# A state-space, expert and attention kernel: early expert loads, woven row sums, reordered attention steps

## The reference, cut to what matters

```
def step(h, inp):
    x_t, dt_t, B_t, C_t = inp
    h = exp(dt_t[..., None] * A[None]) * h + dt_t[..., None] * B_t[:, None, :] * x_t[..., None]
    return h, einsum('bdn,bn->bd', h, C_t) + D_param * x_t
x = x + ssm(xn) + weight[:, None] * expert_of_token(xn)      # layer 0, top 1 of 8
xn = layernorm(x)
scores = g * sem_scores + (1.0 - g) * geo_scores             # layer 1, causal, 16 heads
x = x + softmax(scores) @ v @ wo + shared(xn) + routed_experts(xn)
```

## Time and profile before

| what | value |
|---|---|
| median of 3 runs | 1795.22 us (1791.27 to 1803.44) |
| profiled execution | 1794.59 us, of which 1793.0 us are the span |
| PE busy / PEld busy | 1685.1 us (94%) / 1363.9 us (76%) |
| DVE / ACT / POOL busy | 1181.0 (66%) / 1024.4 (57%) / 784.1 us (44%) |
| granted TensorE clock, mean | 0.975 of 2.4 GHz |
| state steps, about | 77 to 250 us |
| layer-0 experts | 250 to 327 us |
| attention | 367 to 1370 us |
| layer-1 experts and shared expert | 1370 to 1793 us |

### The profile page before, as it was taken

The page is one execution under the profiler, slowest core; times in us unless marked ns, Lnnn a source line. Parts: engine busy times, 40 slices in busy tenths (PEclk is TensorE's granted clock), DMA queues, the critical chain, the costliest instruction groups (busy, mean ns, idle before and its releaser), DMA issues. The chain is left out here.

```text
span 1793.0 us, 33443 instructions
## 1 busy us (share of the span) xinstructions
PE 1685.1 (94%) x9234; PEld 1363.9 (76%) x9234; DVE 1181.0 (66%) x2391; ACT 1024.4 (57%) x2303; POOL 784.1 (44%) x805
## 2 busy tenths in 40 slices
PE   6499989489999999999999999999997999999998
PEld 3365657378888888888888888888886777777787
DVE  6889863687887766766767667667663444344487
ACT  6699934166665656665666666566653444444332
POOL 2599952453334443434443444434550333222374
PEclk9599999699999999999999999999999999999999
DMA  3232339400090100000000000001004999999633
GB/s 127 81 107 94 105 109 309 144 7 1 16 371 11 39 13 22 21 6 26 15 12 20 19 7 29 12 20 38 28 25 151 320 324 313 315 323 322 196 112 100
DMA packets 102555, 193.29 MB, mean 108 GB/s; under 512 B 15700, under 2 KB 59988, under 8 KB 101828
## 3 DMA queue, kind: packets, MB, share of 16 engines
q1 hardware_dynamic: 63300, 125.02, 21.7%
q0 software_dynamic: 17152, 47.67, 8.0%
q10 hardware_dynamic: 22032, 19.73, 3.5%
HBM read 140.84 MB, written 51.51 MB: 107 GB/s over the span
## 5 line engine op out<-in xcount | busy, mean ns | idle before, releaser
L1437 POOL TENSOR_TENSOR sw<-sw,rope_t 64x512 f32<-64x512 f32 x128 | 166.7, 1302 | 521.9 <-ACT sw L1050 492.6
L1079 ACT ACTIVATE pb<-ps,negmax 128x128 f32<-128x128 f32 (+7 forms) x256 | 190.8, 745 | 151.7 <-DVE negmax L1290 150.0
L965 PEld LDWEIGHTS ps<-pt,v 128*128 128x128 f32 x1280 | 242.0, 189 | 42.0 <-DVE xr L1318 4.0
L965 PE MATMUL ps<-pt,v 128*128 128x256 f32 (+1 forms) x1280 | 270.7, 358 | 2.8 <-DVE xr L1318 2.6
L563 POOL DMA_DIRECT2D w2r<-in_w x148 | 77.2, 522 | 314.9 <-PE ps L612 271.4
L1290 DVE TENSOR_REDUCE negmax<-ps 128x1 f32<-128x128 f32 (+7 forms) x256 | 194.0, 758 | 8.8
L646 DVE SCALAR_TENSOR_TENSOR ga<-th,ps 128x176 f32<-128x176 f32 x148 | 50.0, 338 | 225.7 <-ACT th L627 225.7
L1066 ACT COPY pt<-ps 128x512 f32<-128x512 f32 (+3 forms) x384 | 171.6, 484 | 38.7 <-PE ps L955 35.6
L1440 POOL TENSOR_TENSOR t<-t,sw 64x512 f32<-64x512 f32 x128 | 167.8, 1311 | 17.8 <-POOL sw L1437 12.8
L595 PE MATMUL ps<-w13r,xt 128*128 128x352 f32 x496 | 168.6, 463 | 0.0
L955 PE MATMUL ps<-ident,pb 128*128 128x128 f32 x1152 | 167.5, 272 | 0.0
(11 more groups left out here) (246 smaller groups left out, 4000.7 us busy)
## 6 DMA issues: line engine op xcount, KB each, us to landing
w13r<-in_w SPq DMA_DIRECT2D x124, 352.0 KB, 4.8
w2r<-in_w POOLq DMA_DIRECT2D x148, 176.0 KB, 4.8
result<-yy ACTq DMA_DIRECT2D x148, 128.0 KB, 4.5
crow<-c_rows SPq DMA_DIRECT2D x32, 512.0 KB, 3.6
sorted<-zero_tile SPq DMA_DIRECT2D x31, 512.0 KB, 6.1
t<-sorted SPq DMA_DIRECT2D x124, 128.0 KB, 4.0
hc<-in_w SPq DMA_DIRECT2D x24, 352.0 KB, 5.5
wraw<-in_wqk SPq DMA_DIRECT2D x16, 256.0 KB, 2.7
```

The source lines that it names most:

```text
L965: last = pe.matmul(ps[:, 6, c0:2 * P], v[:, j, hd], pt[g % 2][:, j, c0:2 * P], start=j == 0, stop=j == 2 * g + 1)
L1079: act.activation(pb[:, qt % 2, 0:cols], ps[:, bank:bank + 2, :].rearrange("p a n -> p (a n)")[:, 0:cols], ACT.Exp, bias=negmax[:, par, qn: ...
L1437: g.tensor_tensor(sw[64:128, p % 2, :], sw[64:128, p % 2, :], rope_t[64:128, 1, (p // 2) * 512:(p // 2 + 1) * 512], ALU.mult).then_inc(s_t ...
```

## The change

It has three parts, and removes or adds no arithmetic.

1. **Memory and loads.** The layer-0 `w13` ring gets memory of its own, at the end of the stack; the token ring now lies in `zeros`, the tile that the zero fill of `sorted0` reads. SP waits for that fill (R0.zeroed) in place of s_ysum, and makes the table's round trip after the first pair of state steps.
2. **Row sums.** Before the experts nothing is transposed back. The 8 groups stand at the end of the expert steps s = 2 to 7 (one each in 2 to 5, two each in 6 and 7), on TensorE and on VectorE; the wait for s_yT stands at the end of step 1.
3. **Attention.** In odd steps of a first head TensorE makes `values` before `project_out`, and VectorE copies the values before `add_out`. In even steps of a second head VectorE does `output` before `turned`.

```
-        shared_memory = {
-            'w13r0': hc_flat[:, 0:w13_size].rearrange("p (r c n) -> p r c n", r=RING, c=DC),
-            'xs0': hc_flat[:, w13_size:w13_size + RING * D].rearrange("p (r d) -> p r d", r=RING)}
+        shared_memory = {'xs0': zeros[:, 0:RING * D].rearrange("p (r d) -> p r d", r=RING)}
...
+        def rows_in_step(s):
+            if not isinstance(s, int):
+                return ()
+            return {2: (0,), 3: (1,), 4: (2,), 5: (3,), 6: (4, 5), 7: (6, 7)}.get(s, ())
...
                     else:
                         g = qt // 2 - 1
+                        if hh == 0:
+                            m = qt // 2
+                            if m == 0 and b == 0:
+                                pe.wait_ge(s_wvs, hp + 1)
+                            values(m, b, value_fill(pair, m))
                         if g >= 0:
...
                             project_out(it, g, hh)
                         elif not first(it):
                             project_out(it - 1, 3, 1 - hh)
-                        if hh == 0:
...
-                            values(m, b, value_fill(pair, m))
...
-                        if not last:
+                        if hh == 0 and not last:
                             turned(n0 + p, p)
                         if qt > 0:
                             output(it, qt // 2 - 1)
                         elif not first(it):
                             output(it - 1, 3)
+                        if hh == 1 and not last:
+                            turned(n0 + p, p)
...
+                        if hh == 0:
+                            values(qt // 2, value_fill(pair, qt // 2))
                         if qt > 1:
                             add_out(it, qt // 2 - 1, b, hh)
                         elif not first(it):
                             add_out(it - 1, 3, prev_b, 1 - hh)
-                        if hh == 0:
-                            values(qt // 2, value_fill(pair, qt // 2))
...
-            state_pairs(sp, c_row)
-            route_sp(sp, R0)
-            sp.wait_ge(s_ysum, 2 * BATCH * STATES)
+            def first_table(b):
+                if b == 0:
+                    route_sp(sp, R0)
+            state_pairs(sp, c_row, first_table)
+            sp.wait_ge(R0.zeroed, 16 * R0.zero_dmas)
             sp.wait_ge(R0.scattered, 16 * NT)
             experts_sp(sp, R0)
...
+            def add_rows(s):
+                for i in rows_in_step(s):
+                    v.wait_ge(s_yT_ps, i + 1)
...
+            experts_dve(v, R0, add_rows)
...
+            def turn_rows(s):
+                if isinstance(s, int) and s == 1:
+                    pe.wait_ge(s_yT, BATCH * DC)
+                for i in rows_in_step(s):
+                    if i >= 2:
+                        pe.wait_ge(s_yadd, i - 1)
...
+            experts_pe(pe, R0, None, turn_rows)
```

More of the change, by code:

```diff
@@ L131, in ring_buffers @@
         def ring_buffers(r, n, alloc):
-            r.w13 = alloc(f'w13r{n}', [P, RING, DC, 2 * INNER])
+            if n:
+                r.w13 = alloc(f'w13r{n}', [P, RING, DC, 2 * INNER])
             r.w2 = alloc(f'w2r{n}', [IC, RING, 2, D])
@@ L142, in ring_buffers @@
             r.got = alloc(f'got{n}', [P, 4, D])
+            if not n:
+                r.w13 = alloc(f'w13r{n}', [P, RING, DC, 2 * INNER])
         def route_buffers(r, n, e, k, alloc, el, keep_alloc, lw):
@@ L576, in experts_pool, with experts_pe @@
                     load_w2(g, r, i, q)
-        def experts_pe(pe, r, near_end=None):
+        def experts_pe(pe, r, near_end=None, woven=lambda s: None):
             def fn(i, q, kind):
@@ L613, in fn @@
                     last.then_inc(r.dn_done, 1)
+                woven(s)
             tile_steps(pe, r, fn, near_end)
@@ L637, in experts_act, with experts_dve @@
             tile_steps(act, r, fn)
-        def experts_dve(v, r):
+        def experts_dve(v, r, woven=lambda s: None):
             def fn(i, q, kind):
@@ L1035, in body @@
                             project_out(it - 1, 3, 1 - hh)
-                        if hh == 0:
-                            m = qt // 2
-                            if m == 0 and b == 0:
-                                pe.wait_ge(s_wvs, hp + 1)
-                            values(m, b, value_fill(pair, m))
             heads_loop(pe, body)
@@ L1781, in _ @@
             take_sums(1)
-            for i in range(NT // 2):
-                v.wait_ge(s_yT_ps, i + 1)
-                v.tensor_tensor(xr[:, 2 * i:2 * i + 2, :], xr[:, 2 * i:2 * i + 2, :],
-                                ps[:, i % 2, :].rearrange("p (a d) -> p a d", a=2), ALU.add).then_inc(s_yadd, 1)
-            experts_dve(v, R0)
+            def add_rows(s):
+                for i in rows_in_step(s):
+                    v.wait_ge(s_yT_ps, i + 1)
+                    v.tensor_tensor(xr[:, 2 * i:2 * i + 2, :], xr[:, 2 * i:2 * i + 2, :],
+                                    ps[:, i % 2, :].rearrange("p (a d) -> p a d", a=2), ALU.add).then_inc(s_yadd, 1)
+            experts_dve(v, R0, add_rows)
             v.wait_ge(s_yadd, NT // 2)
@@ L2036, in _ @@
                     gather_sum(BATCH * STATES - 2 + q, q, c, False)
-            pe.wait_ge(s_yT, BATCH * DC)
-            for i in range(NT // 2):
-                if i >= 2:
-                    pe.wait_ge(s_yadd, i - 1)
-                for a in range(2):
-                    for c in range(DC):
-                        tt = 2 * i + a
-                        last = pe.transpose(ps[:, i % 2, a * D + c * P:a * D + (c + 1) * P], delta[:, c, tt * P:(tt + 1) * P], ident[:])
-                last.then_inc(s_yT_ps, 1)
-            experts_pe(pe, R0)
+            def turn_rows(s):
[4 more added lines that the diff above has]
+                        pe.wait_ge(s_yadd, i - 1)
+                    for a in range(2):
+                        for c in range(DC):
+                            tt = 2 * i + a
+                            last = pe.transpose(ps[:, i % 2, a * D + c * P:a * D + (c + 1) * P], delta[:, c, tt * P:(tt + 1) * P], ident[:])
+                    last.then_inc(s_yT_ps, 1)
+            experts_pe(pe, R0, None, turn_rows)
             def turn_tokens(q):
```

2 lines of the change are left out of this document (removed).

## The result

| what | before | after |
|---|---|---|
| median, four runs each | 1797.71 us (1791.27 to 1803.44) | 1771.03 us (1765.89 to 1773.82) |
| ratio after / before | | 0.9856, 95% interval 0.9826 to 0.9886 |
| profiled execution | 1794.59 us | 1771.57 us, span 1769.9 us |
| mean granted clock | 0.975 | 0.977 |

The changed kernel is 26.7 us faster by the medians and 23.0 us by the two profiled executions, where 32.3 had been summed. It lies in the range, 8 us above the predicted time.

A forecast was written before the change was run, and what follows sets the result against it. In attention TensorE's own order was taken to set the time, so only its waits could be won. From 1794.6 us, 9.3 at the start and 23.0 in attention gave 1762.3, as a median 1763; range 1750 to 1782.

The forecast's parts named there:

- The start: Layer-0 experts: early loads and woven transposes bring the product of tile 7 9.3 us earlier, bounds 5 and 12 us.
- Loads issued by 237: Hand-over to layer-0 experts: SP issues the weight loads by 237 us, where they went from 250.93.
- The second sum: Start of the experts: VectorE has it at 251.2, before TensorE's new wait at 252.2, so that wait costs nothing.
- the table's trip: States: the table's store and read-back move behind the first pair of states, costed at nothing; at most 14.3 us late.
- Attention, one pair: Waits removed in a pair of heads: 0.66 us in the first head, 0.87 in the second, 1.53 together.
- The count of the pairs: Attention: the pair's gain was taken to repeat in 15 of 16 pairs, 23.0 us in all.
- that rule: Second heads: GpSimd's moved addition may fall onto VectorE's qkl and last 0.75 us longer.
- (a): Rival in attention: waits only move, TensorE then standing behind the exp; 1785 us, no difference; chance 0.13.
- (b): Rival in second heads' even steps: late `turned` delays GpSimd's addition and qkr, 48 us lost against 32; 1811 us; chance 0.05.
- (c): Rival at the start: weights early but first tiles don't gain, 3 of 9.3 us remain; 1769 us; chance 0.14.
- (d): Rival for start and attention: all bounds at their good end, 12 and 32 us won; 1751 us; chance 0.08.
- Everything behind: After the first expert tiles: all to the last store is a chain on them and moves along with their gain.

The follow-up runs named there:

- e2: The changed kernel with the start as before, so only the new attention order; 1782.22 us, ratio 0.9908 to the kernel before.
- e1: The changed kernel with attention in its old order, so only the new start; 1792.81 us against 1799.33 before, ratio 0.9954.
- e5: e1 with delta turned back ahead of the tiles, loads still early; last sum to product of tile 7 24.15 us, 29.95 before.
- e6: e1 with weights and tokens loaded after the last sum as before, transposes still woven; last sum to product of tile 7 33.54 us, 29.95 before.
- e4: The changed kernel with the values in their old place, so only the second heads' swap is left in attention; 1779.25 us.
- e3: The changed kernel with `turned` ahead of `output` everywhere, so only the values come earlier in attention; 1769.1 us.
- e8: The changed kernel with the old attention order in the first three pairs; single time 1767.24 us.
- e7: The changed kernel with `output` before `turned` only in steps 2 and 6 of second heads; single time 1776.81 us.
- e9: The changed kernel with output ahead of the piece in second heads' step 0, taken before ScalarE's copies, plus two matching order edits; 1797.59 us.
- e10: e9 with ScalarE also taking the output ahead of its sw copies in step 2 of second heads; 1789.96 us.
- e11: e7 with ScalarE taking the output ahead of its sw copies in step 2 of second heads; 1782.12 us.
- e12: The same kernel as e7, timed again; median 1781.73 us against 1815.87 of the kernel before beside it, ratio 0.9821.

## Why the prediction was right, and where it was off

**The start: right, and the agreement to 0.1 us in part luck.** Forecast 9.3 us, measured 9.37; but the length before is itself uncertain. Up to the last product of layer 0 the old start takes 70.63 us in the kernel before and 71.69 in e2, the new one 61.09, so that the gain is 9.5 against one and 10.6 against the other. The steps of the forecast hold one by one. Loads issued by 237 (they went at 239.25; 1.6 us of that is the later first sum of this execution, the rest wasn't followed and costs nothing), no idle time ahead of tile 0, 1.40 us to the second product and 2.06 to the third (1.4, and 1.6 + 0.44 with the transposes), 2.92 for a step with four transposes in e1 (254.41 to 257.33; 2.49 + 0.44 forecast), 3.36 for one with eight (268.15 to 271.51; 2.49 + 0.88). The second sum costs nothing, the table's trip costs nothing. What the prediction did not say is that the two edits aren't independent: it took the fall of the clock as a consequence of the late tokens, which e5 and e6 bear out, but the weaving alone would have been a loss of 3.6 us.

**Attention, one pair: right to 0.05 us.** Forecast 1.53, measured 1.49; by place, from the step lengths of a steady pair: first head 0.26 in step 1 and 0.39 in step 3, together 0.65 (0.66 forecast); second head 0.42 in step 0 (0.39), 0.20 in step 3 (0.20) and 0.20 in step 7 (0.28, where the 0.08 of the uncovered load stayed after all). The chain was read rightly too: otl starts 0.04 us after otr's end, and the projection of steps 1 and 3 in second heads is still late.

**The count of the pairs: the term that was mis-sized.** "The pattern repeats over 16 pairs; I count 15" was wrong: the full gain came in 12. Pairs 1 to 3 carry routing work on VectorE (53 of 65 us busy there in pair 2, where a steady pair has 45 of 62), and an instruction of VectorE that moves behind another can cost there: the swap alone lengthens pair 2 by 0.6 us and pair 3 by 1.1 (e4). The gain of the values was to be had in pair 3 (e3); it was lost to the swap. 15 x 1.53 = 23.0 in the sum was 12 x 1.49 + 0.41 + 0.36 = 18.6. The rows of this were to be had from the trace before: its first three pairs are 62.36, 65.06 and 64.38 us long, none like the fourth.

**Pair 1: a case of one port.** The values' order wins 0.4 and 0.2 us in steps 3 and 4 of its first head, and then loses 0.9 and 0.7 us in steps 5 and 6. VectorE and GpSimd there, first before, then after:

```profile
391.60 0.68 DVE L1296 TENSOR_TENSOR qkl<-t,qkr 128x512 fp32r<-128x512 f32 x1
391.70 1.72 POOL L1437 TENSOR_TENSOR sw<-sw,rope_t 64x512 f32<-64x512 f32 x1 [4.65 <-ACT sw L1050]
...
393.45 1.22 DVE L1152 TENSOR_TENSOR xnl<-xnT_b,xnr 128x1024 fp32r<-128x1024 f32 x1
393.50 2.30 POOL L1440 TENSOR_TENSOR t<-t,sw 64x512 f32<-64x512 f32 x1
```

```profile
382.49 1.28 POOL L1446 TENSOR_TENSOR sw<-sw,rope_t 64x512 f32<-64x512 f32 x1 [4.45 <-ACT sw L1057]
382.59 1.73 DVE L1303 TENSOR_TENSOR qkl<-t,qkr 128x512 fp32r<-128x512 f32 x1
...
384.98 0.39 PE L892 MATMUL ps<-wvr,xnr 128*128 128x256 f32 x1 [0.60 <-DVE t L1309]
...
385.06 1.28 POOL L1449 TENSOR_TENSOR t<-t,sw 64x512 f32<-64x512 f32 x1 [1.29 <-DVE t L1309]
385.18 2.25 DVE L1159 TENSOR_TENSOR xnl<-xnT_b,xnr 128x1024 fp32r<-128x1024 f32 x1
...
389.55 0.51 PE L892 MATMUL ps<-xnr,wr 128*128 128x512 f32 x1 [1.10 <-DVE v L1313]
```

In both kernels the same two pairs of instructions meet. Before, VectorE started first by 0.10 and 0.05 us, and GpSimd's took 1.72 and 2.30 in place of 1.28. After, GpSimd started first by 0.10 and 0.12 us, and VectorE's took 1.73 and 2.25 in place of 0.68 and 1.22. The 2.08 us fall on the engine that gives bank 7 back: TensorE stands 0.60 us behind `turned` and 1.10 behind the values' copy (0.39 before), 1.3 of the 1.6 us. The experiments bear it out: in the other profiles with the values in their old place in pair 1 (e1, e4, e5, e6, e8) GpSimd's two take 1.74 to 1.75 and 2.28 to 2.30 us, and in the seven others with the values first (e2, e3, e7, e9 to e12) VectorE's take 1.73 to 1.74 and 2.25 to 2.26. The Trainium skill, SBUF — State Buffer, section Who interferes with whom, has this: a VectorE instruction with two SBUF inputs contends with a GpSimd instruction that reads SBUF for a pair of ports that only one of them holds at a time, and the order of issue decides which one waits. The trace agrees, in both orders: the other one is longer by 0.44 to 1.05 us, where the first still had 0.58 to 1.18 us to run. The prediction weighed that rule for the second heads' addition, where it does not bite (the addition's mean is 1303 ns after); it bites where the two change places.

**The rivals.** (a), the waits only move: fallen; the steady pairs are 1.49 shorter and TensorE's weight loads more densely busy. (b), slower by a late `turned`: its mechanism is there, 43 us of GpSimd waiting behind `turned`, but the timeline of a steady pair's second head shows the room:

```profile
773.67 0.68 DVE L1309 TENSOR_TENSOR t<-ps,rope_t 128x512 f32<-128x512 f32 x1
...
774.43 1.28 POOL L1449 TENSOR_TENSOR t<-t,sw 64x512 f32<-64x512 f32 x1 [2.15 <-DVE t L1309]
...
776.35 0.63 ACT L1092 CAST qkr<-t 128x512 fp32r<-128x512 f32 x1
```

The addition waited 2.15 us and ends at 775.71, and ScalarE takes qkr 0.64 us later. Where the room is used up by routing, it costs 1.2 us in pair 3, through the exp behind it on VectorE's mask. (c), first tiles without gain: fallen, all 1.35 us long. (d), all bounds good: fallen; 8.4 us of waiting for otl remain in second heads, and the three orders of e9 to e11 that went for them cost more than that.

**The total.** Of the 9.3 us between 32.3 and 23.0, attention accounts for 4.4 (the count of pairs, with the port in pair 1 and the swap in pair 3), the two stages outside the change for 6.2, and the rest of layer 0 and the gather, 1.2 us shorter, for -1.2. "Everything behind" the tiles "moves along" holds only up to these differences between executions, for which the sum had no term.

## What to carry to other kernels

Read a repeating pattern's gain from one period, but count the periods from their measured lengths: a period that is longer before the change may have another limit and is to be read by itself. Here two of the three longer pairs gained nothing and one 0.6 us, where a steady pair gained 1.5. When an in-order engine gets an instruction moved behind one that waits, look for the longest thing that ever stands behind it in any period; the steady one may hide what the few loaded ones pay. And edits that fill and remove the same idle time must be tried together: here the weaving lost 3.6 us alone and won 3.6 more on top of the early loads.

## What the runs showed of the hardware

Three that had not been expected. Whether VectorE or GpSimd starts 0.1 us ahead of the other decided in pair 1 who pays: 1.5 us on GpSimd before, 2.1 us on VectorE after. In e9 1.28 in place of 0.68 us for qkl came back in every second pair. A stage whose DMA engines are full (share 1.02 to 1.04 in the three windows shown) took from 314.5 to 328.3 us over 14 profiles, 4%, for the same 99.2 MB and, in e7 and e12, for the same kernel with 2.8% between them, while attention repeated to 0.1 us in those two (apart from them it has the 0.4 us of pair 1's step 0): what is won in such a stage must be timed in many runs, and what is won in the other can be read from one trace. And the stretch ahead of the first sum has two lengths, 1.0 us and more apart, by whether the granted clock rises at 75 us; neither belongs to one of the kernels.
